# First squares by two queues, other engines for parts of the weight splits, and the last experts added on TensorE, in a conditioned feed-forward kernel

## The reference

```python
w = weights[conditions]
hidden = jnp.einsum('bct,bcd->bdt', x, w)
logits = jnp.einsum('bsh,he->bse', hidden, gate_w)
routing_weights, _ = jax.lax.top_k(logits, 2)
h = jnp.einsum('bsh,hi->bsi', hidden, up_w)          # 256 -> 1024
h = jnp.square(jax.nn.relu(h))
shared_out = jnp.einsum('bsi,ih->bsh', h, down_w)    # 1024 -> 256
moe_out = jnp.einsum('bsh,hd->bsd', hidden, expert_weight) * routing_weights.sum(-1, keepdims=True)
y = shared_out + moe_out
out = x + (y - y.mean()) * rsqrt(y.var() + 1e-5) * ln_gamma + ln_beta
```

## Time and profile before

| | us |
|---|---|
| three runs, median (lowest to highest) | 232.68 (231.88 to 232.74) |
| the profiled execution | 231.9 |
| its span, first to last instruction | 230.2 |
| of that outside the span | 1.7 |
| busy: PE / DVE / POOL / ACT | 222.6 / 149.3 / 133.5 / 107.0 |
| first up product starts | 9.19 |
| last down product starts | 225.01 |
| last `result` made (1.08 from 226.93) | 228.01 |

### The profile page before, as it was taken

One profiled execution on the slowest core, in us unless ns is written; L12 is line 12 of the kernel. 1 busy time (PEld: TensorE's weight loads), 2 busy tenths in 40 slices (PEclk: granted clock), 3 DMA queues, 4 the chain that ended last, 5 costly groups with the idle time before them and its releaser, 6 DMA issues.

```text
span 230.2 us, 3997 instructions
## 1 busy us (share of the span) xinstructions
PE 222.6 (97%) x1264; PEld 191.6 (83%) x1264; DVE 149.3 (65%) x380; ACT 107.0 (46%) x188; POOL 133.5 (58%) x130
## 2 busy tenths in 40 slices
PE   7899999999999999999999999999999999999991
PEld 2697888888888888888888888888888888888991
DVE  6385865666565666766656665656567666666885
ACT  2397945444435444444463444354444444444100
POOL 3729973657546665477536575466653675466422
PEclk9999999999999999999999999999999999999998
DMA  5783313030503020000200002000200002000111
GB/s 187 215 240 122 86 23 101 8 98 7 187 8 98 8 91 5 0 0 3 91 0 3 0 0 94 3 0 0 77 17 0 1 0 95 0 0 0 57 59 68
DMA packets 16889, 11.81 MB, mean 51 GB/s; under 512 B 6628, under 2 KB 16356, under 8 KB 16868
## 3 DMA queue, kind: packets, MB, share of 16 engines
q1 hardware_dynamic: 15140, 9.91, 14.4%
q10 hardware_dynamic: 1312, 1.59, 2.2%
q0 software_dynamic: 416, 0.05, 0.2%
HBM read 7.35 MB, written 4.19 MB: 50 GB/s over the span
## 4 chain that ended last, share of the span: by engine, by line
PE 89%; DVE 3%; issue 2%; DMA 2%; POOL 1%; POOLq 1%; ACT 1%; DVEq 0%
PE up_ps L304 36%; PE down_ps L390 25%; PE down_ps L392 13%; PE hid_ps L277 5%; PE moe_ps L406 3%; PE moe_ps L408 3%; PE moe_ps L407 3%; DMA wd<-in_L_cond_weights_dram 1%; POOL sq_lo L619 1%; POOLq L188 1%; DVE square L511 1%; DVE up_lo L566 1%; DMA cond_row<-in_itok_B_dram 1%; ACT up_hi L455 0%; PE down_ps L277 0%
## 5 line engine op out<-in xcount | busy, mean ns | idle before, releaser
L619 POOL TENSOR_TENSOR sq_lo<-square,sq_hi 128x512 fp32r<-128x512 f32 x64 | 83.8, 1313 | 61.8 <-DVE square L511 61.8
L390 PE MATMUL down_ps<-down_hl,sq_hi 128*128 128x512 f32 x248 | 88.7, 392 | 0.0
L392 PE MATMUL down_ps<-down_hl,sq_lo 128*128 128x256 f32 x248 | 69.6, 280 | 0.0
L511 DVE SCALAR_TENSOR_TENSOR square<-up_ps,relu 128x512 f32<-128x512 f32 x64 | 44.0, 688 | 35.9 <-ACT relu L449 34.7
L390 PEld LDWEIGHTS down_ps<-down_hl,sq_hi 128*128 128x128 f32 x248 | 46.5, 188 | 10.6
L449 ACT ACTIVATE relu<-up_ps 128x512 f32<-128x512 f32 x64 | 38.1, 596 | 32.7 <-PE up_ps L304 32.7
L304 PE MATMUL up_ps<-hid_hi,up_hi 128*128 128x512 f32 (+1 forms) x136 | 53.0, 393 | 0.1
L304 PE MATMUL up_ps<-hid_hi,up_lo 128*128 128x512 f32 (+1 forms) x136 | 51.1, 379 | 0.0
L392 PEld LDWEIGHTS down_ps<-down_hl,sq_lo 128*128 128x128 f32 x248 | 46.7, 188 | 2.4
L451 ACT ACTIVATE sq_hi<-relu 128x512 fp32r<-128x512 f32 x64 | 40.6, 634 | 2.0
L304 PE MATMUL up_ps<-hid_lo,up_hi 128*128 128x512 f32 (+1 forms) x136 | 40.2, 380 | 0.0
(11 more groups left out here) (51 smaller groups left out, 202.8 us busy)
## 6 DMA issues: line engine op xcount, KB each, us to landing
x_sb<-in_x_dram SPq DMA_DIRECT2D x7, 512.0 KB, 3.9
out_dram<-result SPq DMA_DIRECT2D x7, 512.0 KB, 3.0
wd<-in_L_cond_weights_dram SPq DMA_DIRECT2D x110, 4.0 KB, 1.6
result<-in_L_ffn_up_w_dram ACTq DMA_DIRECT2D x2, 512.0 KB, 4.3
x_sb<-in_L_ffn_down_w_dram SPq DMA_DIRECT2D x2, 512.0 KB, 4.9
x_sb<-in_x_dram ACTq DMA_DIRECT2D x1, 512.0 KB, 3.6
out_dram<-result SPq DMA_DIRECT2D x4, 128.0 KB, 1.7
eg_raw<-L_ffn_expert_weight_dram SPq DMA_DIRECT2D x1, 256.0 KB, 3.8
```

Source lines behind the costliest of these rows:

```text
L390: pe.matmul(dst[:, :], a_hi, down_hl[:, c, :, :].rearrange("p s t -> p (s t)"), start=(c == 0), stop=False)
L392: mm = pe.matmul(dst[:, T:2 * T], a_lo, down_hl[:, c, 0, :], start=False, stop=(c == CH - 1))
L511: dve.scalar_tensor_tensor(square[:, c % 2, :], up_ps[c % UPB][:, :], 0.0, relu[:, c % 2, :], ALU.max, ALU.mult).then_inc(square_done, 1)
L619: pool.tensor_tensor(sq_lo[:, j % 2, c, :], square[:, c % 2, :], sq_hi[:, j % 2, c, :].bitcast(f32), ALU.subtract).then_inc(sq_lo_done, 1)
```

## The change

It has these parts; the names are those of the diff.

- **Squares of block 0.** The first 8 (half 0) are issued by SP and ACT alone, 4 each, with a semaphore for each group of 4. The other 8 go to POOL (8 to 12, after it has also waited for the later conditions) and SP (13 to 15, after a second read of registers).
- **Loads ahead of them.** ACT's first two transfers are half of x of block 0 and two chunks of up (256 KB each, were 512 KB each). After its squares it issues two more chunks of up and the other half of x. SP issues the last four chunks of up (512 KB), after its squares and ahead of eg.
- **TensorE's order at the start.** Group 0 is conditioned when its squares are there. Half 0 of chunks 0 and 1 is finished (with the `hid_lo` products) before chunk 2 is begun; after the conditioning of half 1 stand half 0's rest of chunk 2 and chunk 3.
- **Other engines.** DVE rounds the last four chunks of up (a copy, ahead of the second half's `hid_lo`). POOL splits the down quarter 0, both parts, ahead of its first `sq_lo`. Quarter 1 is split by ACT and DVE after chunk 4 of block 0.
- **Order in block 0.** `round_at(0)` is (4, 5): half 1 of block 1's conditioning stands after chunk 5. `add_beta` of block 0 moves into block 1.
- **The last tile.** Its scaled experts are split in hi (ACT) and lo (DVE, `moe_rest`) and added to `down_ps` by two products with an identity, which POOL makes (`affine_select`, from `ones` by DVE). DVE's addition is gone; moments and centring read PSUM.

```diff
-SPLIT_DOWN_AT = {5: 2, 7: 3}
-QUEUES = 3
+SPLIT_DOWN_AT = {4: 1, 5: 2, 7: 3}
+BY_SP, BY_ACT, BY_POOL, BY_SP_LATER = range(0, 8, 2), range(1, 8, 2), range(8, 13), range(13, 16)
...
         def round_at(j):
-            return (4, 6) if j == 0 else (2, 4)
+            return (4, 5) if j == 0 else (2, 4)
...
+            values = conditions(mybir.EngineType.SP, BY_SP)
             sp.wait_ge(wd_zeroed[0], 1)
             for b, value in values:
+                sp.dma_start(square_of(b), weights_of(value)).then_inc(wd_first_landed[b // Q], 16)
+            values = conditions(mybir.EngineType.SP, BY_SP_LATER)
+            for b, value in values:
+                sp.dma_start(square_of(b), weights_of(value)).then_inc(wd_later_landed[0], 16)
+            load_up(sp, 2)
             sp.dma_start(eg_raw[:, :, 0:T], expert_w.rearrange("(k p) h -> p k h", p=P)).then_inc(eg_landed, 16)
...
             def first_chunks():
                 conditioning_first(0)
-                for c in range(FIRST - 1):
-                    first_rounded(c, 0)
+                first_rounded(0, 0)
+                first_rounded(1, 0)
+                first_rest(0, 0)
+                first_rest(1, 0)
+                first_rounded(2, 0)
                 conditioning_first(1)
-                first_rounded(FIRST - 1, 0)
-                for c in range(FIRST):
-                    first_rest(c, 0)
+                first_rest(2, 0)
+                first_rounded(3, 0)
+                first_rest(3, 0)
...
+                if last_tile(j, t) and half == 0:
+                    pe.wait_ge(identity_ready, 1)
+                    pe.wait_ge(moe_rest_done, 1)
+                    for part in range(2):
+                        pe.matmul(dst[:, 0:T], identity[:, :], moe_hl[:, part, :], start=(part == 0), stop=False)
...
+            load_x_first(act, 0)
+            load_up(act, 0)
...
+            load_up(act, 1)
+            load_x_first(act, 1)
             split_up(0)
+            hidden_first(0, 0)
+            hidden_first(0, 1)
             split_up(1)
-            for half in range(2):
-                for k in range(K):
-                    hidden_first(half, k)
-            split_up(2)
+            hidden_first(1, 0)
+            hidden_first(1, 1)
...
-            split_down(0)
-            split_down(1)
...
+            dve.wait_ge(up_landed[2], 16)
+            dve.tensor_copy(up_hi[:, :, split_cols(2)], up_raw[:, :, split_cols(2)]).then_inc(up_hi_ready, 1)
+            hidden_first(1, 0)
+            hidden_first(1, 1)
...
+            def split_down_first():
+                pool.wait_ge(down_landed[0], 16)
+                pool.tensor_copy(down_hl[:, down_chunks(0), 0, :], down_raw[:, down_chunks(0), :]) \
+                    .then_inc(down_first_hi, 1)
+                pool.wait_ge(down_first_hi, 1)
+                pool.tensor_tensor(down_hl[:, down_chunks(0), 1, :], down_raw[:, down_chunks(0), :],
+                                   down_hl[:, down_chunks(0), 0, :].bitcast(f32), ALU.subtract) \
+                    .then_inc(down_first_ready, 1)
```

More of the change, by code:

```diff
@@ L83, in adaln_ffn @@
         moe = sb("moe", [P, 2, TILES, T])
+        moe_hl = sb("moe_hl", [P, 2, T], f32r)
+        ones = sb("ones", [P, P])
+        identity = sb("identity", [P, P], f32r)
         y_half = sb("y_half", [P, T])
@@ L191, in conditions @@
             return list(zip(batches, values))
-        def in_turn(queue):
-            return range(queue, TILES * Q, QUEUES)
-        def count_hw(half):
-            return 16 * sum(b // HALF_BLOCK == half for q in range(2) for b in in_turn(q))
-        def count_pool(half):
-            return 16 * sum(b // HALF_BLOCK == half for b in in_turn(2))
         def square_of(batch):
@@ L209, in weights_of, with load_up, load_x_first @@
             return cond_w[bass.ds(row, 1), :, :].rearrange("s c d -> (s c) d")
+        def load_up(queue, part):
+            cols = split_cols(part)
+            queue.dma_start(up_raw[:, :, cols], up_rows[:, :, cols]).then_inc(up_landed[part], 16)
+        def load_x_first(queue, half):
+            part = slice(TILES // 2 * half, TILES // 2 * (half + 1))
+            queue.dma_start(x_sb[:, part, :], x_rows[:, part, :]).then_inc(x_first_landed[half], 16)
         block = ctx.enter_context(nc.Block())
@@ L453, in split_up @@
             def split_up(part):
-                act.wait_ge(up_landed[part // 2], 16)
+                act.wait_ge(up_landed[part], 16)
                 act.activation(up_hi[:, :, split_cols(part)], up_raw[:, :, split_cols(part)], ACT.Copy) \
@@ L577, in _ @@
             dve.memset(wd[:, TILES:GROUPS, :], 0.0).then_inc(wd_zeroed[1], 1)
+            dve.memset(ones[:, :], 1.0).then_inc(ones_ready, 1)
             split_up(0)
+            hidden_first(0, 0)
+            hidden_first(0, 1)
             split_up(1)
-            for half in range(2):
-                for k in range(K):
-                    hidden_first(half, k)
+            dve.wait_ge(up_landed[2], 16)
+            dve.tensor_copy(up_hi[:, :, split_cols(2)], up_raw[:, :, split_cols(2)]).then_inc(up_hi_ready, 1)
+            hidden_first(1, 0)
+            hidden_first(1, 1)
             split_up(2)
@@ L653, in _ @@
                         split_square(j, c)
-                    if j < BLOCKS and c in (CH - 4, CH - 2):
+                    if j == 1 and c in (0, 2):
+                        add_beta(0, c // 2)
+                    if 0 < j < BLOCKS and c in (CH - 4, CH - 2):
                         add_beta(j, (c - CH + 4) // 2)
+                    if j == BLOCKS - 1 and c == CH - 1:
+                        pool.wait_ge(ones_ready, 1)
+                        pool.affine_select(identity[:, :], ones[:, :], pattern=[[-1, P]], compare_op=ALU.is_equal,
+                                           fill=0.0, base=0, channel_multiplier=1).then_inc(identity_ready, 1)
                     if j > 0 and c % 2 == 1:
```

99 lines of the change are left out of this document (55 added, 44 removed).

## The result

| | before | after |
|---|---|---|
| runs beside each other: median (lowest to highest) | 232.28 us (231.88 to 232.74, 4 runs) | 235.59 us (234.64 to 236.19, 4 runs) |
| ratio, 95% interval | | 1.0151 [1.0132, 1.0170] |
| profiled execution, span | 231.9, 230.2 us | 235.64, 234.0 us |
| last product of TensorE starts | 225.01 | 229.38 |

The kernel became slower by 3.3 to 3.5 us. That lies in the range of the prediction (232.9 to 236.4) and above its 234.5. The span grew by 3.8 us: chunk 7 starts 4.2 us later, and the end gives 0.4 back.

What follows compares the result with a forecast made beforehand. TensorE was taken as the bound, busy 222.6 of 230.2 us, leaving only start and end open. +2.0 us at the moved conditioning half and -0.2 at the end gave +1.8: 234.5 us, 8-in-10 range 232.9 to 236.4.

Steps and rivals of the forecast that it cites:

- chunk 7 starts: TensorE's up product of chunk 7 in block 0: start at 26.3 us against 24.30, +2.0 us.
- the end: Last tile: VectorE's addition goes (-0.46 us), two products come (+0.24), -0.2 us; bounds -0.25 and 0.
- first up product: TensorE's first up product: at 8.9 us, 0.3 earlier, bounds 0 to 0.45; no way for the gain to reach the end.
- M: Start of ScalarE's first scaled experts: 20.49 us before, forecast 20.5 as before, bounds 19.2 and 22.3.
- rest of quarter 1 on VectorE: VectorE's remainder of down quarter 1, put ahead of `hid_lo`: claimed to fit beside ScalarE's `hid_hi`.
- gap of TensorE: TensorE standing still for `hid_lo` right behind the experts of tile 1: 2.1 us.
- conditioning half, chunk 6: TensorE's second conditioning half of block 1, then chunk 6's up product, after the wait: 0.92 and 1.40 us.
- The main step: Block 1's second conditioning half, moved ahead of chunk 6's up product, waits for `hid_lo`: +2.0 us, reaching the end.
- The squares of block 1: Issued by SP 1.2 to 1.6 us later; first conditioning half may wait half a microsecond, costing nothing behind M.
- a clock below 1.00 after the gap: Sign that the forecast is wrong: TensorE's granted clock under 1.00 behind its wait for `hid_lo`.
- a rival with 0.06: Clock falls in TensorE's new 2.1 us gap: at most 2.9 us lost, some 2.3 likely, 236.7 us; chance 0.06.
- the likeliest case: M near 20.5, TensorE waits some 2 us for `hid_lo`, +1.8 us in sum, 234.5 us; chance 0.59.

Runs made afterwards that it cites:

- the run with the split moved: Changed kernel with round_at(0) = (4, 6), down quarters 1 to 3 after chunks 5, 6, 7, and POOL's down split behind its fourth `sq_lo`: 231.44 us, 0.9982.
- the two runs with filling products: Changed kernel with ten, then five, unread TensorE products ahead of block 1's waiting second conditioning half: 234.52 us, 1.0106, and 234.48 us, 1.0114.
- another, which had one more wait of 0.63 us ahead of the experts: The kernel before with only round_at(0) changed from (4, 6) to (4, 5): 235.15 us, ratio 1.0132.
- both moves undone: Changed kernel with block 1's second conditioning half back behind chunk 6 and down quarters 1 to 3 after chunks 5, 6, 7; alone: 232.06 us, 1.0012.

## Why the prediction was right in its direction and short in its size

| step of the prediction | forecast | measured |
|---|---|---|
| first up product | 8.9 (0.3 earlier) | 9.24 (0.05 later) |
| down half 0 landed, POOL begins | 14.4, 14.5 | 14.80, 14.85 |
| POOL's copy, subtraction | 0.8, 1.4 | 0.61, 1.29 |
| `sq_lo` of chunk 0 starts; M | 16.8; 20.5 | 16.80; 20.48 |
| TensorE leaves the experts of tile 1 | M + 1.36 (by the next start) | M + 1.64 (end of the last product) |
| rest of quarter 1 on VectorE | 0.69, beside `hid_hi` | 1.41, ends behind it |
| `hid_lo` ends | M + 3.46 | M + 4.19 |
| gap of TensorE | 2.1 | 2.60 |
| conditioning half, chunk 6 | 0.92, 1.40 | 1.73, 2.06 |
| chunk 7 starts | M + 5.83, +2.0 | M + 8.03, +4.2 |
| the end | -0.2 | -0.4 |

**Right.** The main step held, with its place and its reason: the half ahead of chunk 6 waits for `hid_lo`, and nothing behind it gives the loss back. M stayed where it was, because POOL took over what ScalarE and VectorE had lost; the pairs of copy and M show that it hangs on POOL, and the run with the split moved shows it once more, M falling to 19.56. Its first `sq_lo` no longer took 1.61 us, and from there to M it was 3.7 us as worked out. The squares of block 1 did make TensorE wait 0.70 us at 18.2, and it cost nothing in the changed kernel, as forecast, since M stood behind it. The claim that a gain of the first products can't reach the end held too: with twelve warm-up products they came 1.1 us earlier, for nothing.

**Luck.** That `sq_lo` and M came within 0.02 us is partly luck: down landed 0.4 later than forecast, and copy and subtraction were 0.3 shorter; M lies between 20.31 and 21.36 in the eight traces with POOL's quarter first. The range, too, holds the measured time for another reason than its own. Its upper bound came from loads that land late (M up to 22.3). M was where it was forecast, for which the sum gives +1.8 us; the median rose by 3.3 and the profiled execution by 3.7, and what filled the range are the two terms below. One of the prediction's own signs of being wrong, a clock below 1.00 after the gap, is there.

**The step that was mis-sized: VectorE beside POOL.** The sum took 0.69 us for the rest of the quarter from a row in which VectorE was alone or POOL paid. Beside `sq_lo` it is 1.41. That is 0.72 of the 2.2 us that the forecast of chunk 7 was short. The trace of before had the price in it. There VectorE makes the same subtraction for quarters 2 and 3, beside POOL's `add_beta`, VectorE first and then POOL:

```profile
24.30 1.05 DVE L571 TENSOR_TENSOR down_hl<-x_sb,down_hl 128x512 fp32r<-128x512 f32 x1
...
28.11 1.47 DVE L571 TENSOR_TENSOR down_hl<-x_sb,down_hl 128x512 fp32r<-128x512 f32 x1
```

```profile
23.52 1.28 POOL L628 TENSOR_TENSOR x_sb<-x_sb,beta_b 128x512 f32<-128x512 f32 x1
...
27.72 1.30 POOL L628 TENSOR_TENSOR x_sb<-x_sb,beta_b 128x512 f32<-128x512 f32 x1
```

The earlier trace rows is the same thing from the other side: POOL's `sq_lo` took 1.61 instead of 1.29 when VectorE had begun the rest of quarter 1 just before it, and VectorE kept its time:

```profile
16.25 0.68 DVE L571 TENSOR_TENSOR down_hl<-x_sb,down_hl 128x512 fp32r<-128x512 f32 x1
```

I read it as something about the first of its kind and asked neither what stood beside it nor who would pay the next time. The rows answer both: the two take turns, and the one that starts second pays.

| second to start | it starts | the first one ends | the second ends | behind it |
|---|---|---|---|---|
| VectorE, quarter 2, before | 24.30 | 24.80 | 25.35 | 0.55 |
| VectorE, quarter 3, before | 28.11 | 29.02 | 29.58 | 0.56 |
| VectorE, quarter 1, changed kernel | 22.66 | 23.52 | 24.07 | 0.55 |
| POOL, `sq_lo` of chunk 0, before | 16.48 | 16.93 | 18.09 | 1.16 |

In the fourteen traces all 36 such subtractions of VectorE that began beside POOL end 0.55 us behind POOL's instruction, and all 19 of POOL that began beside VectorE's end 1.15 to 1.17 behind that; the one that began first took its usual time (0.68 to 0.69, 1.26 to 1.31). So the price is what the other has still to do, less 0.14 us, and it could have been worked out: `sq_lo` of chunk 4 began at M + 1.77 in the trace of before (22.26) and lasts 1.30, the rest of quarter 1 then ends at M + 3.62 and `hid_lo` at M + 4.2. Measured is M + 4.19. Instructions of VectorE with one input in PSUM (the squares, `hid_lo`) kept their 0.67 to 0.69 us beside POOL in every trace here. The Trainium skill says so: "GPSIMD Engine Reference", section "Key points", has GpSimd sharing its SBUF interfaces with VectorE, with contention for instructions with two SBUF inputs. The traces agree, with 1.41 to 0.69 us.

**The chance that was too small: the clock.** It cost 1.47 us in the profiled run (0.81 on the half, 0.66 on chunk 6), the rest of the 2.2. The prediction had it as a rival with 0.06, at most +2.9 us and some 2.3 likely. The mistake is twofold. It was treated as an alternative to the likeliest case, though it can only come with it. And its chance was read from the one place where the clock fell after a long idle time, with no row for gaps between 0.5 and 2.7 us; between "did nothing" and "fell" the sum should have taken an open chance. It fell in three of the four runs of the changed kernel (mean clock 0.990 to 0.992; the fourth has 0.999 and is the fastest, 234.64 us). Without it the kernel is at 1.011, as the two runs with filling products show: +2.0 by the sum, +0.7 for VectorE, -0.4 at the end make 2.3, and 2.5 to 2.6 were measured.

**Small ones.** The warm-up took 6.37 us instead of 5.86 for the same products, so the first up product gained nothing; it took 4.93 to 6.37 in the sixteen-product traces, which is more than the 0.3 us at stake. The end gained 0.4, not 0.2: POOL's `rstd` was 0.17 shorter, which the sum didn't have. Six squares in 2.86 us are 0.48 each, not 0.51; down was issued at 8.99 where 9.1 was forecast, so nothing hung on it. POOL's copy took 0.61 us, which is the estimate that the prediction set beside its own 0.8.

**What is open.** Which gaps make the clock fall. A gap of 1.35 to 1.38 us (one trace each) did nothing in twelve runs of three kernels, and one of 1.37 us did in four of four runs of another, which had one more wait of 0.63 us ahead of the experts; gaps of 2.6 and 2.9 us did in three and two of four. For runs without a trace this is read from the mean clock and the time. Neither the gap's length nor the idle time of the microseconds around it sorts these, and no run here tells what does.

## What to carry to other kernels

When an order is changed, look at what the moved instruction waits for and at what covered that wait; a one-line move ahead of its cover cost 1.4 us here, and the clock as much again. Price a gap of TensorE with the clock as an open chance on top, not as a rival. For an instruction of VectorE with two inputs in SBUF, ask what POOL will be doing when it starts, and add what is left of that. Work that is moved to the engine on which the chain hangs is not moved off the path: the split of down belonged behind POOL's `sq_lo`, not ahead of them, and with that, its loads behind the squares, and both moves undone, the change's other parts make the kernel 0.5% faster than before; 0.2% of it is the end's.
